# Pool normalises two of the four opening tiles of a decoder layer instead of VectorE

## The reference

```
x = x + attn(LN(x))          causal, 32 query heads, 8 key/value groups, head size 16
x = x + xattn(LN(x), ctx)    8 heads over the channels, keys and values from ctx
x = x + ffn(LN(x))           weights rounded to -1, 0, 1, activations to 8 bits, inner size 2048

LN:   (x - mean) / sqrt(var + 1e-5)
attn: q = x Wq^T, k = x Wk^T, v = x Wv^T;  softmax(q k^T / 4, causal) v;  then Wo^T
```

## Time and profile before

| | us |
|---|---|
| three timed runs: median | 808.04 |
| lowest, highest | 806.4, 808.13 |
| profiled execution, its own time | 809.84 |
| its span, first to last instruction | 807.8 |

### The profile page before, as it was taken

How to read it: one execution, slowest core, us unless ns; L and a number is a source line. 1 busy time by engine, 2 the same in 40 slices (tenths; PEclk the granted TensorE clock), 3 DMA queues, 4 the chain that set the end, 5 groups by cost and what they waited for, 6 DMA issues and landing times.

```text
span 807.8 us, 14447 instructions
## 1 busy us (share of the span) xinstructions
PE 763.5 (95%) x4342; PEld 407.6 (50%) x4342; DVE 642.9 (80%) x1921; ACT 480.2 (59%) x844; POOL 424.3 (53%) x437
## 2 busy tenths in 40 slices
PE   8999999999979999998999699999899999999988
PEld 6777544444444444443877455554444344444433
DVE  7676888898878888881689778888975888888884
ACT  4666566676656776775455766666666455444452
POOL 5554479999994000001334577988878344432331
PEclk9999999999999999999999999999999999999999
DMA  8898664544431122101387655655552335333435
GB/s 291 302 377 289 205 194 129 156 129 152 155 104 51 51 66 62 51 26 29 123 277 244 190 158 162 172 169 163 163 157 62 54 77 105 75 84 78 86 79 130
DMA packets 112028, 113.61 MB, mean 141 GB/s; under 512 B 70640, under 2 KB 82160, under 8 KB 108880
## 3 DMA queue, kind: packets, MB, share of 16 engines
q1 hardware_dynamic: 109600, 99.66, 43.1%
q0 software_dynamic: 1840, 12.98, 4.7%
q10 hardware_dynamic: 512, 0.07, 0.1%
HBM read 81.26 MB, written 20.51 MB: 126 GB/s over the span
## 4 chain that ended last, share of the span: by engine, by line
PE 18%; DVE 15%; issue 6%; SPq 5%; POOL 4%; DMA 2%; ACT 2%; ACTq 0%; DVEq 0%; POOLq 0%
PE r_pn L1590 4%; DVE r_h L1431 3%; POOL r_h L1200 3%; PE r_p L1542 3%; PE r_p L1576 3%; PE r_p L1577 3%; PE r_pd L1600 1%; DVE r_hpart L1439 1%; PE r_p L1633 1%; DVE r_amax L1462 1%; PE r_pd L1650 1%; DVE r_zn L1460 1%; SPq L1016 1%; SPq L1010 1%; ACT r_silu L1307 1%
## 5 line engine op out<-in xcount | busy, mean ns | idle before, releaser
L787 ACT ACTIVATE b_probs<-ab_j 128x512 f32<-128x512 f32 (+1 forms) x352 | 176.6, 560 | 32.3 <-PE ab_j L852 13.5
L147 DVE CUSTOM_DVE_ANT_0 b_junk<-ab_t,mask_qk 128x128 bf16<-128x128 f32 (+2 forms) x243 | 108.8, 485 | 27.2 <-PE ab_t L127 26.9
L852 PE MATMUL ab_j<-qs,ks 98*128 98x512 bf16 (+1 forms) x352 | 122.4, 362 | 6.3 <-DMA qs<-mrow 5.2
L147 DVE CUSTOM_DVE_ANT_0 b_junk<-ab_e,mask_qk 128x256 bf16<-128x256 f32 (+2 forms) x237 | 104.1, 482 | 6.1 <-PE ab_e L127 5.6
L1268 ACT ACTIVATE r_probs<-r_p 128x512 f32<-128x512 f32 x128 | 74.0, 594 | 52.3 <-PE r_p L1577 51.0
L1376 DVE TENSOR_REDUCE r_mx<-r_p 128x1 f32<-128x512 f32 x128 | 86.4, 678 | 18.5 <-PE r_p L1542 17.3
L1167 POOL TENSOR_TENSOR r_halves<-r_probs 128x1024 f32<-128x1024 f32 x32 | 76.7, 2397 | 15.0 <-ACT r_probs L1268 13.0
L870 PE MATMUL ab_pv<-b_probs,v 128*32 128x512 f32 (+3 forms) x1024 | 75.5, 436 | 0.0
L1633 PE MATMUL r_p<-wg,r_zt 128*128 128x512 bf16 x256 | 65.8, 380 | 4.0 <-DMA r_zt<-r_zq 1.9
L1129 POOL MEMSET r_ql<- 64x2048 f32 x1 | 1.8, 1799 | 128.4 <-POOLq L237 128.4
L127 PE MATMUL ab_e<-ks,qs 96*128 96x128 bf16 (+3 forms) x269 | 64.1, 301 | 5.1 <-DMA ks<-k_parts 1.6
(11 more groups left out here) (167 smaller groups left out, 1668.1 us busy)
## 6 DMA issues: line engine op xcount, KB each, us to landing
r_k<-in_ctx SPq DMA_DIRECT2D x64, 128.0 KB, 2.7
r_qh<-x_normed_high SPq DMA_DIRECT2D x64, 128.0 KB, 2.7
qs<-q_parts SPq DMA_DIRECT2D x32, 192.0 KB, 3.2
q_parts<-a_parts SPq DMA_DIRECT2D x15, 384.0 KB, 6.0
a_wst<-in_w_gate SPq DMA_DIRECT2D x4, 1024.0 KB, 7.6
a_wst<-in_w_up SPq DMA_DIRECT2D x4, 1024.0 KB, 9.8
a_wst<-in_w_down SPq DMA_DIRECT2D x4, 1024.0 KB, 8.0
qs<-q_parts SPq DMA_DIRECT2D x32, 128.0 KB, 2.7
```

The lines of the kernel that those rows point to most:

```text
L147: best = nc.vector.tensor_tensor_reduce(out=junk[:, 2 * (st.use[i, k] % slots) + n, 0:w], in0=bank[:, c:c + w], in1=keep["mask_qk"][:, SEQ ...
L787: nc.scalar.activation(pblock(j % 2, kb)[:, j0:j0 + nj, c:c + w], p2[(NE * j + n) % BANKS2][:, 0:nj * w].rearrange("p (j c) -> p j c", j=n ...
L852: last = nc.tensor.matmul(bank, ks[0:STACK + 2, s, kb * P:(kb + 1) * P], qs[0:STACK + 2, s, j0:j0 + nj, kb * P + c:kb * P + c + w], start= ...
```

## The change

Pool gets a function `normalise` and calls it for the third and fourth tile of the first batch, right behind the deviation of the tile. VectorE keeps the first two. A new semaphore, `normed_pool`, counts Pool's two; `normed` counts VectorE's, and is two smaller from then on, so all that wait for it wait for two less. TensorE's `turn` waits for the new semaphore at these two tiles, and `load_x` for both.

```diff
@@ -296,6 +296,7 @@
     x0_in, w_in = m.sems("x0_in", TPB), {t: m.sem(f"w_in_{t}") for t in ("wk", "wq", "wv")}
     wof_in = m.sem("wof_in")
     consts, ident_z = m.sem("consts"), m.sem("ident_z")
+    normed_pool = m.sem("normed_pool")
     ones_set = m.sem("ones_set")
     w_high = m.sem("w_high")
     w_split = m.sem("w_split")
@@ -333,7 +334,8 @@
             sp.dma_start(wst[:, w, :], ffn_d[w][:, bass.ds(FF * b, FF)]).then_inc(wst_in[w], 16)
 
         def load_x(b):
-            sp.wait_ge(normed, TPB * b)
+            sp.wait_ge(normed_pool, 2)
+            sp.wait_ge(normed, TPB * b - 2)
             sp.dma_start(x[:], x_d[b]).then_inc(x_in, 16)
 
         def store_parts(b, n):
@@ -400,7 +402,7 @@
             nc.gpsimd.tensor_scalar(veps[:, tiles], mv[:, tiles, 1], LN_EPS, None, ALU.add).then_inc(veps_done, 1)
             pool.wait_ge(veps_done, n + 1)
             if due(TPB * b):
-                pool.wait_ge(normed, TPB * b)
+                pool.wait_ge(normed, TPB * b - 2)
             nc.gpsimd.tensor_tensor(rstd[:, tiles], veps[:, tiles], keep["minus_half"][:, tiles], ALU.pow).then_inc(rstd_done, 1)
 
         def part(g):
@@ -416,8 +418,15 @@
             pool.wait_ge(part_m, g + 1)
             nc.gpsimd.tensor_tensor(parts[:, t, 2, :], rest[:, g % 2, :], parts[:, t, 1, :], ALU.subtract).then_inc(part_l, 1)
 
+        def normalise(t):
+            pool.wait_ge(rstd_done, t + 1)
+            pool.sem_inc(keep["pool_passed"], 1)
+            nc.gpsimd.tensor_scalar(xn[:, t, :], x[:, t, :], mv[:, t, 0:1], rstd[:, t:t + 1], ALU.subtract, ALU.mult).then_inc(normed_pool, 1)
+
         for t in range(TPB):
             deviations(t, 0, slice(t, t + 1))
+            if t >= 2:
+                normalise(t)
         pool.wait_ge(lo_done, TPB)
         nc.gpsimd.memset(keep["v"][:, :, :, HDIM:2 * HDIM], 1.0).then_inc(padded, 1)
         pool.wait_ge(padded, 1)
@@ -548,10 +557,9 @@
             if t == TPB - 1:
                 split(0, 0)
             gather(0, t)
-            if t > 0:
+            if 0 < t < 3:
                 first_norm(t - 1)
         split(0, 1)
-        first_norm(TPB - 1)
         split_weights(0)
         split(0, 2)
         split(0, 3)
@@ -613,7 +621,10 @@
         pe.wait_ge(consts, 1)
 
         def turn(b, t):
-            pe.wait_ge(normed, TPB * b + t + 1)
+            if b == 0 and t >= 2:
+                pe.wait_ge(normed_pool, t - 1)
+            else:
+                pe.wait_ge(normed, t + 1 if b == 0 else TPB * b + t - 1)
             if b > 0:
                 pe.wait_ge(lo_done, TPB * b + t - 1)
             for k in range(KD):
```

## The result

The changed kernel is slower: a median of 810.12 us over 22 runs against 807.29 us over 22 runs of the kernel before, a ratio of 1.0033 with a 95% interval of 1.0021 to 1.0046, that is +2.7 us (1.7 to 3.7). The forecast was 808.2 us, at most 809.5, and no change that can be measured, so it was wrong. The profiled executions don't show the loss in their length: 807.8 us of span before, 807.6 after. Single executions of either kernel differ by more than the effect (804.74 to 810.23 us before, 807.57 to 814.59 after), so I read the profile for where the opening went, not for the total.

A forecast was written before the change was run, and what follows sets the result against it. The opening was taken to be bound by wq's arrival and, without slack, the second batch's x load. VectorE's relief 0 plus Pool's longer chain +0.12 us on 808.04 gave 808.2 us, range 806.3 to 809.5.

The forecast's parts named there:

- What ends last in the opening: Opening: wq's arrival ends last before the projections; the second batch's x load has no slack and delays TensorE equally.
- the 0.98 us I gave: TensorE's idle of 0.34 and 0.64 us at 21.74 and 23.04 us, taken to swallow a late first matmul.
- the arrival of wq: Before the first projection: ScalarE's rounding waits for wq's DMA until 11.06 us, leaving the fourth tile's normalising 0.28 us to spare.
- VectorE's relief is worth nothing: Opening: two normalisings leaving VectorE bring its subtractions forward by tenths of a microsecond, up to one; valued at 0.
- I take 0.69 us for each: Pool's two moved normalisings: 0.69 us each, from its feed-forward normalising row; 0.62 and 1.01 kept as ends.
- the rest of my sum: Pool's chain from 8.38 us: two normalisings, epsilon 0.22, power 0.57, gaps 0.08; ends at 10.72 against 10.60, +0.12 us.
- 0.08 us between dependent instructions on Pool: Pool in the opening: a dependent instruction starts 0.08 us after the one before it ends.
- The port: Pool's last normalising beside VectorE's weight subtraction: an exclusive SBUF lock would make the sum +0.3 to +0.7 us; not used.
- The clock in the opening: Rival: TensorE's clock falls at 12.95 us, 1.7 us lost, 0.98 given back; 808.9 us, chance 0.03.
- The collision near 228: Pool's last weight load meets SyncE's loads of the maxima; TensorE waits 3.86 us. Rival without it: 802.6 us, chance 0.06.
- The 5.6 us: Gain if the collision near 228 us went away: 3.9 us of TensorE's wait plus 1.7 us of lowered clock.
- The chances: Whole kernel: faster by over 1.6 us 0.08, slower by over 1.6 us 0.12, within 0.80.

The follow-up runs named there:

- second profile of the same program: The kernel before, run again without an edit; ratio 1.0012 (0.9991 to 1.0034).
- the kernel with the quick kind: The changed kernel with Pool's two normalisings as x * rstd + mean instead of (x - mean) * rstd, for its time alone; ratio 1.0019 to the kernel before.
- the reordering: VectorE's first weight subtraction put behind that of tile 2; on the changed kernel with x * rstd + mean ratio 0.9999, with x * rstd + shift 1.0024.
- the last form: The changed kernel with Pool normalising as x * rstd + shift and VectorE's first weight subtraction behind that of tile 2; ratio 1.0024 (1.0006 to 1.0042).
- the late-load kernel: The kernel before with the load of the second batch's x waiting for the first batch's fourth subtraction; ratio 1.0052 (1.0032 to 1.0073).
- the kernel with scale and shift: The changed kernel with Pool normalising as x * rstd + shift, shift = -mean * rstd made by Pool first; ratio 1.0023 (1.0001 to 1.0044).
- that with the late projection: The kernel before with the first projection waiting for four weight tiles instead of one; ratio 1.0017 (0.9994 to 1.0041).
- Pool's last load 34 us earlier: The kernel before with Pool's 48 weight roundings as add and multiply instead of a single subtraction; ratio 0.9999 (0.9980 to 1.0019).
- the first experiment: The kernel before plus 30 Pool tensor_scalar instructions, ten kinds, three of each, that feed nothing; 812.64 us, one run.

## Why the prediction was wrong, step by step

- **What ends last in the opening.** Right for the load of x, which has no slack: +2.95 us at its issue, +2.96 us at the third turned tile, +2.7 us in time. The first projection has slack, and more than the 0.98 us I gave: of 1.9 us of delay 1.7 were given back. That the arrival of wq is its last wait held for one execution only. In the second profile of the same program ScalarE rounded the wq tile at 10.58 without waiting for a DMA, and the first matmul came at 12.59.
- **VectorE's relief is worth nothing.** Right. In the kernel with the quick kind VectorE is early by nearly a microsecond (its first weight subtraction at 9.52 instead of 10.51), and the ratio is 1.0019 or, with the reordering, 0.9999.
- **"I take 0.69 us for each, the median of the nearest row, and keep 0.62 and 1.01."** This is the step that failed: it is 2.09 us, twice the upper end. I matched the row by engine, shape, type and operands, not by its two operations. The row multiplies and adds; the change subtracts and multiplies. With 2.09 in its place and the rest of my sum as it stood, the fourth tile ends at 8.38 + 2.09 + 0.01 + 0.22 + 0.08 + 0.57 + 0.08 + 2.09 = 13.52 us, +2.92, and the forecast would have been 811.0 us, slower; put on the 22 runs' 807.29 it is 810.2, and 810.12 was measured. The warning stood in the view from which the earlier trace rows is taken: Pool's weight rounding, 128x512 as well, a single subtraction. The rows of the kernel before, with the limiting that follows it:

```profile
L761 POOL TENSOR_SCALAR wg<-b_wst 128x512 bf16<-128x512 f32 x16 | 23.8, 1489 | 1.4
...
L763 POOL TENSOR_SCALAR wg<-wg 128x512 bf16<-128x512 bf16 x16 | 9.8, 613 | 1.3
```

  Two rows of one shape, 1489 ns here and 618 in the earlier trace rows, 2.4 times as long, are a sign that the operations matter. I had both rows before me and used only the quick one. As an upper end the slow row would have given 12.32 us, +1.72, 809.8 us: slower as well, but still short, for no row of before holds the kind that takes 2.09.
- **0.08 us between dependent instructions on Pool.** Right between epsilon and power, wrong behind the power: 0.22. It adds 0.28 us over the two, so the sum becomes 2.92 + 0.28 = 3.20 us, and counted from the third tile's power the load was 3.18 us late. That the plain sum, 13.52, meets the 13.54 of the profile is luck: the opening ran 0.23 us ahead.
- **The port.** The sentences on the Trainium skill's "SBUF — State Buffer" gave +0.3 to +0.7 us. For Pool's small instructions the trace agrees: in the kernels with the quick kind the power took 1.11 us beside the weight subtraction, and 0.57 once the subtraction stood later. With the slow kind it does not: Pool's normalising ran from 8.29 to 10.38 and VectorE's weight subtraction from 9.32 for 0.68 us within it, and neither was longer than alone (2.09 against 2.07, 0.68 against 0.68). The rule's lock for a whole instruction is not what this pair shows, and the measurement decides. Two other overlaps cost little: Pool's normalising of 10.27 took 2.22 us where the subtraction of 9.83 was still running, and in the last form VectorE's subtraction of 11.67 took 0.85 us beside Pool's quick normalising of 11.22.
- **The clock in the opening.** I gave the fall 3 in 100 because I thought of 0.12 us more idle. With the real gaps of 1.94 and 2.51 us it fell, at about 11.0, at the end of the four transposes between the two. It cost nothing by itself here, since the idle ahead of the second batch took it; in the late-load kernel a fall had nothing behind it and cost some 1.4 us. What decides stays open: behind 2.00 us of idle in the kernel with scale and shift, and behind 2.41 in that with the late projection, the clock stayed up.
- **The collision near 228.** I argued from three runs within 1.7 us that it belongs to every execution. Twenty-two runs spread over 5.5 us, and the profiles show the wait at 4.14, 2.07 and 0.22 us. Three runs were too few for that sentence. How much of the spread it explains isn't shown. The 5.6 us that I put on its going away aren't there to be won: with Pool's last load 34 us earlier the long wait is gone from the profile, and the time is the same to within 1.6 us.
- **The chances.** No case of mine held an instruction over 1.01 us, so 0.12 for slower rested on collisions only.

Left open: why a pair of addition and multiplication is quick and a single addition or a pair with a subtraction isn't, what makes the granted clock fall, and whether the 22 runs' +2.7 us and the shift of 2.96 us differ at all.

## What to carry to other kernels

Before work is moved to another engine, price it by a row with the same engine, shape, type and the same operations. Two rows of one shape that differ twofold say that something in the form matters. If no row has the operations, even the slowest of that shape is no upper end (1.49 us here, against 2.09 measured): time the very instruction, as the first experiment does. On Pool (x - m) * r took nearly three times x * r + s (2.09 against 0.76 us), so carry the shift, not the mean; here even that form lost 1.9 us. In an opening, find the instruction that lets the next batch's load go: a delay ahead of it was paid at the end, as closely as could be measured, while a late start of the first matmuls was given back up to about 1.7 us.

## What the runs showed of the hardware

- Pool, tensor_scalar on 128x512 f32: 0.62 to 0.77 us for a pair of one addition and one multiplication, 1.49 to 1.56 for a single addition or subtraction, 1.92 to 2.07 for a pair with a subtraction, away from the opening. With a bf16 output, 618 ns for the first kind and 1489 for a single subtraction.
- A single addition on Pool costs more than an addition and a multiplication: adding a constant took 1497 ns, adding it and multiplying 617.
- Pool's power on one column took 1.11 us instead of 0.57 when a VectorE subtraction of two SBUF operands began in the same moment; its 128x1 epsilon took 0.58 instead of 0.23 when begun 0.17 us into one.
- TensorE's granted clock fell to 0.50 after idle of 1.94 us and four transposes, and after 2.73 us of idle and four transposes in the middle of the projections. It stayed at 1.00 behind idle of 2.00 and of 2.41 us in two other kernels, so the length of one idle stretch did not decide.
